# A fused attention and expert layer: state products in 32 by 32 pieces, scores a round earlier, half the keys turned outside TensorE, convolution taps shared by two engines

## The chip, the cores and the metric

The kernel runs on one core of a Trainium2 chip. The metric is the device time of one execution in microseconds (us); lower is better. The version before takes 1308.19 us, the median of three runs (1307.94 to 1309.42).

## The reference

The input is `x`, 8 sequences of 2048 tokens with 256 channels, in fp32. The output is `x` plus two branches that both read the normalised input.

```python
xn = layernorm(x)
# attention, 16 heads of 16, causal and linear (no softmax)
q, k, v = split(xn @ wqkv);  q, k = relu(q), relu(k)
kv  = cumsum(k[..., :, None] * v[..., None, :], axis=2)       # a 16x16 state per head
num = einsum('bhnd,bhnde->bhne', q, kv)
den = einsum('bhnd,bhnd->bhn', q, cumsum(k, axis=2)) + 1e-5
attn = (num / den) @ wo
# experts: top 2 of 8 by a sigmoid router; 4 are gated MLPs (256 -> 128 -> 256)
routed = sum_e cw[:, e] * ((silu(xn @ Wg[e]) * (xn @ Wu[e])) @ Wd[e])
routed += (cw[:, 4] + cw[:, 6]) * xn + cw[:, 7] * relu(xn)
shared = causal depthwise convolution of xn, 4 taps, + conv_b
out = x + attn + routed + shared
```

## The kernel before

**Tiling.** A sequence is cut into 4 batches of 512 tokens, a batch into 4 tiles of 128 tokens; there are 32 batches in all. The program is written out without loops on the chip: each engine has its own list of instructions in a fixed order, and semaphores tie the lists together. Nothing reorders the work but the order in which the code is written.

**One batch on TensorE.** `batch(s, j, left)` goes through these steps:

1. For each tile t: `gate_up(t)` (12 products of 512 columns) for expert t of all 512 tokens, then `numerators(t)`: a sum into the running state (`state_sum`, line 429), the masked scores times the values (line 466), another state sum, and the state times the query (line 482). After tile 0 the scores of the batch's tiles 2 and 3 are made (`scores(s, j, 0, 1)`, line 415).
2. `heads(s, j, 1)` makes values, keys and queries of the next batch, and turns its keys from channels by tokens into tokens by channels with eight 128 by 128 transposes (line 397) for the state sums. ScalarE copies them out to `ktok`.
3. For each tile, `output(t)`: the convolution turned back (line 488), attention times `wo`, hidden times `Wd`. Before tile 3 stand the scores of the next batch's tiles 0 and 1 (`scores(s, j, 1, 0)`) and its first state sum.

A weight or an input in fp32 is split in a high and a low part, so a matrix product is three passes (line 343). Products of attention (lines 415, 429, 466, 482) are plain fp32; the trace has each of these as two matmuls.

**PSUM.** Eight banks: four hold the scores (`SB[0..3]`, which also take the key and query projections and the transposes), three form a ring for everything in the tile loop, one holds the state. So scores can be written only when the masks of the scores before them are done.

**State times query.** Per 64 tokens the state is 256 channels by 16 for each head. VectorE's `blocks` (line 902) spreads it over a block-diagonal `state_bd` of 128 by 256, and TensorE multiplies it by `qT` in four products of 128 rows and 64 columns. `blocks` reads the state bank, so the next state sum waits for it (`s_bd`).

**Convolution.** From the fourth batch on, xn is turned in 32 by 32 blocks on VectorE (line 854) and the blocks are put in place by 32 small DMAs (SP, line 311), not by TensorE. The convolution starts with a ScalarE instruction pair (`first_tap`, line 654), and VectorE adds the other three taps with two multiply-adds each (line 916), after tiles 1, 2 and 3. TensorE needs the sum at `output(0)`.

**Engine queues.** ScalarE's list in a tile is `silu(t)`, `high_hid(t-1)`, `high_y(t)`. TensorE's `numerators(t)` waits for `silu(t)`, and `gate_up(t+1)` waits for VectorE's `hid` and `yT` of tile t. At the start of a batch TensorE's list also holds 38 waits on a semaphore that has long been set (`FILL`).

## Time and profile before

| | |
|---|---|
| median of 3 runs | 1308.19 us |
| the profiled execution, device time | 1308.92 us |
| its span (first to last instruction) | 1307.1 us |
| TensorE busy | 1287.2 us (98%) |
| VectorE busy | 1144.3 us (88%) |
| GpSimd busy | 830.8 us (64%) |
| ScalarE busy | 707.8 us (54%) |
| HBM traffic | 54 GB/s over the span |

The profiled execution is 1.8 us longer than its span and 0.7 us above the median. TensorE is written as PE (and PEld for its weight loads), VectorE as DVE, ScalarE as ACT, GpSimd as POOL and SyncE, which issues DMAs, as SP. In a timeline row the first number is the start, the second the length; rows of one kind are merged (x16 is sixteen instructions). A merged row's length reaches to the end of the last one, which is later than the start of the next row, since matmuls overlap; so steps are measured from start to start. "[0.54 <-X]" is idle time before a row and what ended it. A letter q behind an engine means its sequencer.

### The profile page before, as it was taken

What the parts mean: (1) busy time and instruction counts of PE and PEld (TensorE: products, weight loads), DVE (VectorE), ACT (ScalarE), POOL (GpSimd) and SP (SyncE); (2) the same over time, 40 slices, a digit from 0 to 9 for tenths busy, and PEclk for the clock granted to TensorE, in tenths of its full rate; (3) what the DMA queues carried; (4) which work ended last, traced back from release to release, by engine and by line L of the source; (5) the groups of instructions that cost most, each with busy time, mean ns of one, the idle gap of its engine ahead of it and who ended that gap; (6) DMA issues with size and microseconds to landing.
All of it is one profiled execution on the core that took longest, in us unless ns stands there. A gap on an engine that the chain in (4) does not pass through costs nothing.

```text
span 1307.1 us, 55818 instructions
## 1 busy us (share of the span) xinstructions
PE 1287.2 (98%) x24160; PEld 1116.5 (85%) x24160; DVE 1144.3 (88%) x2686; ACT 707.8 (54%) x1487; POOL 830.8 (64%) x673
## 2 busy tenths in 40 slices
PE   5999999999999999999999999999999999999998
PEld 4888888888888888888888888888888888888887
DVE  7988898888898888988888988889888889888885
ACT  5645655455654456554555544565545555445552
POOL 2676665765666756657656667566576566675554
PEclk9999999999999999999999999999999999999999
DMA  5012212222222222222222222221222222222211
GB/s 185 14 56 73 78 50 51 80 78 78 65 61 56 79 78 79 51 51 81 78 79 64 67 51 78 78 78 51 51 80 78 79 64 67 51 78 63 61 35 34
DMA packets 175860, 88.54 MB, mean 68 GB/s; under 512 B 135552, under 2 KB 171264, under 8 KB 171520
## 3 DMA queue, kind: packets, MB, share of 16 engines
q1 hardware_dynamic: 174912, 83.97, 22.6%
q8 instruction: 191, 3.13, 1.0%
q10 hardware_dynamic: 704, 1.01, 0.2%
q14 instruction: 53, 0.43, 0.1%
HBM read 53.18 MB, written 17.04 MB: 54 GB/s over the span
## 4 chain that ended last, share of the span: by engine, by line
PE 95%; DVE 3%; POOL 1%; issue 1%; ACT 0%; DMA 0%; DVEq 0%; POOLq 0%
PE ring L343 51%; PE scores L343 17%; PE ring L466 7%; PE ring L482 6%; PE scores L415 5%; PE state_sum L429 4%; PE ring L488 2%; PE scores L397 2%; DVE sm L895 1%; POOL xn L731 0%; DMA x_t<-in_L_attn_x_dram 0%; PE scores L352 0%; POOL rstd L722 0%; DVE stats L819 0%; POOL x_t L748 0%
## 5 line engine op out<-in xcount | busy, mean ns | idle before, releaser
L757 POOL TENSOR_TENSOR hid<-hid,cwb 128x512 f32<-128x512 f32 x128 | 166.4, 1300 | 181.8 <-DVE hid L924 181.0
L916 DVE SCALAR_TENSOR_TENSOR cT<-xT,conv_ws,cT 128x512 f32<-128x512 f32 x192 | 275.1, 1471 | 0.0
L745 POOL TENSOR_TENSOR x_t<-x_t,same 128x1024 f32<-128x1024 f32 x32 | 76.9, 2404 | 254.9 <-ACT same L618 254.9
L639 ACT ACTIVATE sg<-ring 128x512 f32<-128x512 f32 x128 | 76.6, 599 | 268.5 <-PE ring L343 268.5
L343 PE MATMUL ring<-xl,wgu_h 128*128 128x512 f32 x512 | 213.1, 416 | 0.0
L761 POOL TENSOR_TENSOR hl<-hid,hh 128x512 fp32r<-128x512 f32 x128 | 208.8, 1632 | 0.0
L343 PE MATMUL ring<-xh,wgu_l 128*128 128x512 f32 x512 | 201.0, 393 | 0.3 <-issue 0.3
L343 PE MATMUL ring<-xh,wgu_h 128*128 128x512 f32 x512 | 200.5, 392 | 0.0
L569 ACT ACTIVATE yh<-yT 128x256 fp32r<-128x256 f32 x128 | 53.5, 418 | 246.7 <-DVE yT L933 246.7
L902 DVE TENSOR_TENSOR state_bd<-state_sum,tables_s 128x256 f32<-128x256 f32 x248 | 104.0, 419 | 93.8 <-PE state_sum L429 90.6
L895 DVE TENSOR_TENSOR sm<-scores,causal_s 128x512 f32<-128x512 f32 x256 | 157.7, 675 | 6.0 <-PE scores L415 5.0
L343 PE MATMUL ring<-wd_l,hh 128*128 128x256 f32 x496 | 139.3, 281 | 0.0
L343 PE MATMUL ring<-wd_h,hh 128*128 128x256 f32 x496 | 139.1, 280 | 0.0
L343 PE MATMUL ring<-wd_h,hl 128*128 128x256 f32 x496 | 139.0, 280 | 0.0
L766 POOL TENSOR_TENSOR yl<-yT,yh 128x256 fp32r<-128x256 f32 x128 | 135.3, 1057 | 0.0
L466 PE MATMUL ring<-sm,vp 64*32 64x64 f32 x8192 | 122.2, 225 | 0.0
L343 PEld LDWEIGHTS ring<-xl,wgu_h 128*128 128x128 f32 x512 | 96.1, 188 | 26.1 <-issue 5.5
L343 PEld LDWEIGHTS ring<-xh,wgu_l 128*128 128x128 f32 x512 | 96.4, 188 | 23.1 <-issue 0.8
L343 PEld LDWEIGHTS ring<-xh,wgu_h 128*128 128x128 f32 x512 | 96.6, 189 | 16.6
L466 PEld LDWEIGHTS ring<-sm,vp 64*32 64x32 f32 x8192 | 101.6, 105 | 2.8 <-issue 2.8
L343 PE MATMUL scores<-xh,wqk_h 128*128 128x512 f32 x256 | 100.2, 392 | 0.0
L343 PE MATMUL scores<-xl,wqk_h 128*128 128x512 f32 x256 | 100.2, 391 | 0.0
(134 smaller groups left out, 3453.4 us busy)
## 6 DMA issues: line engine op xcount, KB each, us to landing
cwb<-cw_rows SPq DMA_DIRECT2D x32, 1024.0 KB, 4.6
x_t<-in_L_attn_x_dram SPq DMA_DIRECT2D x32, 512.0 KB, 4.2
out_dram<-x_t SPq DMA_DIRECT2D x31, 512.0 KB, 2.9
xT<-qks_tok SPq DMA_DIRECT2D x896, 16.0 KB, 1.8
cw_rows<-cwt SPq DMA_DIRECT2D x128, 2.0 KB, 1.4
sm<-in_L_attn_wqkv_dram ACTq DMA_DIRECT2D x2, 384.0 KB, 5.0
sm<-in_L_ffn_Wg_dram SPq DMA_DIRECT2D x2, 256.0 KB, 3.8
sm<-in_L_ffn_Wu_dram SPq DMA_DIRECT2D x2, 256.0 KB, 4.6
```

The source lines that it names most:

```text
L343: ins = mm(dst, lhs, rhs, start=first and n == 0, stop=final and n == len(passes) - 1, skip_group_check=not (first and final))
L415: ins = mm(SB[f][h * HALF:(h + 1) * HALF, at_:at_ + P], kT[rows, g, n0:n0 + HALF], qp[rows, g, :, n0:n0 + HALF], start=True, stop=True)
L466: mm(NB2[t % 2][h][BLK * m:BLK * m + BLK, gs], window, sm[toks, t // 2, t % 2, 2 * pair + par, :], start=par == 0 and g == 0, stop=False, ...
L482: ins = mm(NB2[t % 2][h][rows, g * HALF:(g + 1) * HALF], state_bd[:, n % 4, cols], qT[:, g, n0:n0 + HALF], start=False, stop=True, skip_gr ...
L639: act.activation(sg[:, :], GB[t % 2], ACT.Silu).then_inc(s_sg, 1)
L745: pool.tensor_tensor(xb, xb, same[:, :, :], ALU.add).then_inc(s_base1, 1)
L757: pool.tensor_tensor(hid[:, e, :], hid[:, e, :], cwb[:, e, :], ALU.mult).then_inc(s_hid, 1)
L761: pool.tensor_tensor(hl[:, e, :], hid[:, e, :], hh[:, e, :].bitcast(F32), ALU.subtract).then_inc(s_hl, 1)
L766: pool.tensor_tensor(yl[:, :, t * P:(t + 1) * P], yT[:, t % 2, :, :], yh[:, :, t * P:(t + 1) * P].bitcast(F32), ALU.subtract).then_inc(s_y ...
L895: dve.tensor_tensor(heads, SB[f][:, :].rearrange("p (t a n) -> p t a n", a=2, n=HALF), causal2_s[:, :].unsqueeze(1).unsqueeze(1).to_broadc ...
L902: dve.tensor_tensor(state_bd[:, n % 4, :].rearrange("p (g m n) -> p g m n", g=C, m=PPG), ST.unsqueeze(2).to_broadcast([P, C, PPG, BLK]), s ...
L916: ins = dve.scalar_tensor_tensor(out=cT[:, c, :], in0=xT[:, third(s, j, 0), c, LEAD - HALO + n:LEAD - HALO + n + BT], scalar=conv_ws[:, c, ...
```

## The change

1. **State times query.** `blocks` writes `state_ph`, 128 by 64: the state times a mask that separates the two heads of a pair. TensorE multiplies each 32 by 32 diagonal block on its own: 4 products per group of 128 channels and 64 tokens in place of 2. Each reads another 32 rows and writes another 32 partitions of one bank.
2. **Scores.** The scores of tiles 2 and 3 of a batch move from behind `numerators(0)` to behind the last `output(3)` of the batch before, and their masks on VectorE with them.
3. **Keys.** Of the eight key transposes, TensorE keeps the four of tiles 0 and 1. The other half is turned in 32 by 32 blocks by two VectorE instructions (`turn_keys`, into `hid[:, 2]`) and put in place by 16 small DMAs from SP. Three waits on `ktok_in` and `s_hl` guard this.
4. **Taps.** Where the next batch's xn goes by blocks, ScalarE multiplies (`tap_terms`, into the PSUM banks `SB[0:2]`) and VectorE only adds. The key projection, which uses these banks, now waits for `s_conv`.
5. **DMA issue.** Of the 32 DMAs that place xn, SP keeps 24; ScalarE issues 8, four behind each of two `tap_terms`.
6. The 38 waits (`FILL`) are removed.

```diff
-                            for w in range(2):
-                                rows = slice(w * HALF, (w + 1) * HALF)
-                                cols = slice(g * P + w * HALF, g * P + (w + 1) * HALF)
-                                ins = mm(NB2[t % 2][h][rows, g * HALF:(g + 1) * HALF], state_bd[:, n % 4, cols],
-                                         qT[:, g, n0:n0 + HALF], start=False, stop=True, skip_group_check=True)
+                            for m in range(PPG):
+                                rows = slice(BLK * m, BLK * m + BLK)
+                                ins = mm(NB2[t % 2][h][rows, g * HALF:(g + 1) * HALF], state_ph[rows, n % 4, g, :],
+                                         qT[rows, g, n0:n0 + HALF], start=False, stop=True, skip_group_check=True)
...
-                    for t in range(T):
+                    for t in range(T // 2 if k else T):
                         ins = nc.tensor.transpose(KTB[g][:, t * P:(t + 1) * P], kT[:, g, t * P:(t + 1) * P],
...
+                if k and by_blocks(s, j, k):
+                    pe.wait_ge(s_conv, at(s, j, HALO, HALO))
                 for g in range(C):
                     project(KB[g][:, :], D + g * P).then_inc(s_kp, 1)
...
+            def turn_keys(s, j, k):
+                for g in range(C):
+                    dve.wait_ge(s_kT, at(s, j, C, k * C + g + 1))
+                dve.wait_ge(s_hl, at(s, j, T, 3))
+                for t in range(2):
+                    ins = dve.transpose(kb[:, :, t, :, :].rearrange("p a g i -> p g a i"), ...
+                ins.then_inc(s_kturn, 1)
...
-                dve.tensor_tensor(state_bd[:, n % 4, :].rearrange("p (g m n) -> p g m n", g=C, m=PPG), ...
+                dve.tensor_tensor(state_ph[:, n % 4, :, :].rearrange("p g (a d) -> p g a d", a=2),
+                                  ST.rearrange("p g (a d) -> p g a d", a=2),
+                                  parity_s[:, :].unsqueeze(1).unsqueeze(3).to_broadcast([P, C, 2, HD]), ALU.mult
+                                  ).then_inc(s_bd, 1)
...
+                def tap_terms(n):
+                    if n == 1:
+                        act.wait_ge(s_sm, at(s, j, U * ROWS, U * ROWS))
+                    else:
+                        act.wait_ge(s_conv, at(s, j, HALO, n - 1))
+                    for c in range(C):
+                        first = LEAD - HALO + n
+                        ins = act.activation(TB[c][:, :], xT[:, third(s, j, 0), c, first:first + BT], ACT.Copy,
+                                             scale=conv_ws[:, c, n:n + 1])
+                    ins.then_inc(s_tapped, 1)
...
+                    for c in range(C):
+                        ins = dve.tensor_tensor(cT[:, c, :], TB[c][:, :], cT[:, c, :], ALU.add)
+                    ins.then_inc(s_conv, 1)
```

**The order on TensorE, from the last product of a batch to the second expert of the next.** `wd` rows end `output(3)`, `wgu` rows are `gate_up`, `scores` is line 415 (441 in the changed kernel). Before:

```order
L343 MATMUL ring<-wd_h,hl 128x256
L343 MATMUL ring<-xl,wgu_h 128x512 [waits tables_in,s_out]
...
L429 MATMUL state_sum<-vp,ktok 32x32 [waits s_bd]
L429 MATMUL state_sum<-vp,ktok 32x32 x7
L482 MATMUL ring<-qT,state_bd 64x64 [waits s_bd]
L482 MATMUL ring<-qT,state_bd 64x64 x3
L482 MATMUL ring<-qT,state_bd 64x64 [waits s_bd]
L482 MATMUL ring<-qT,state_bd 64x64 x3
L415 MATMUL scores<-qp,kT 64x128 [waits s_sm]
L415 MATMUL scores<-qp,kT 64x128 x31
L343 MATMUL ring<-xl,wgu_h 128x512 [waits s_gu]
```

In the changed kernel:

```order
L365 MATMUL ring<-wd_h,hl 128x256
L441 MATMUL scores<-qp,kT 64x128 [waits s_sm]
L441 MATMUL scores<-qp,kT 64x128 x31
L365 MATMUL ring<-xl,wgu_h 128x512 [waits s_out]
...
L458 MATMUL state_sum<-vp,ktok 32x32 [waits s_bd]
L458 MATMUL state_sum<-vp,ktok 32x32 x7
L510 MATMUL ring<-qT,state_ph 32x64 [waits s_bd]
L510 MATMUL ring<-qT,state_ph 32x64 x7
L510 MATMUL ring<-qT,state_ph 32x64 [waits s_bd]
L510 MATMUL ring<-qT,state_ph 32x64 x7
L365 MATMUL ring<-xl,wgu_h 128x512 [waits s_gu]
```

The 32 score products stand ahead of `gate_up(0)` instead of behind `numerators(0)`, and the group of 4 state products has become a group of 8.

**The order on VectorE, at the end of a batch and the start of the next.** `sm` rows are the masks of the scores, `x_t` rows add `output(t)`. Before:

```order
L976 TENSOR_TENSOR x_t<-ring,x_t 128x256 [waits s_op,s_base2]
L895 TENSOR_TENSOR sm<-scores,causal_s 128x4x128 [waits s_s]
L895 TENSOR_TENSOR sm<-scores,causal_s 128x4x128 x3
L902 TENSOR_TENSOR state_bd<-state_sum,tables_s 128x256 [waits s_st]
L976 TENSOR_TENSOR x_t<-ring,x_t 128x256 [waits s_op,s_base2]
L902 TENSOR_TENSOR state_bd<-state_sum,tables_s 128x256 [waits s_st]
```

In the changed kernel:

```order
L1060 TENSOR_TENSOR x_t<-ring,x_t 128x256 [waits s_op,s_base2]
L962 TENSOR_TENSOR sm<-scores,causal_s 128x4x128 [waits s_s]
L962 TENSOR_TENSOR sm<-scores,causal_s 128x4x128 x3
L969 TENSOR_TENSOR state_ph<-state_sum,tables_s 128x64 [waits s_st]
L1060 TENSOR_TENSOR x_t<-ring,x_t 128x256 [waits s_op,s_base2]
L962 TENSOR_TENSOR sm<-scores,causal_s 128x4x128 [waits s_s]
L962 TENSOR_TENSOR sm<-scores,causal_s 128x4x128 x3
L969 TENSOR_TENSOR state_ph<-state_sum,tables_s 128x64 [waits s_st]
```

A second set of masks now follows the last `x_t` of a batch, and the first set is what TensorE's moved scores wait for (`s_sm`).

**The order on ScalarE, in tiles 1 and 2 of a batch.** `sg` is `silu`, `hh` and `yh` are `high_hid` and `high_y`. Before:

```order
L639 ACTIVATE sg<-ring 128x512 [waits s_gu,s_gp]
L569 ACTIVATE hh<-hid 128x512 [waits s_hid]
L569 ACTIVATE yh<-yT 128x2x128 [waits s_y]
L639 ACTIVATE sg<-ring 128x512 [waits s_gu,s_gp]
L569 ACTIVATE hh<-hid 128x512 [waits s_hid]
```

In the changed kernel:

```order
L673 ACTIVATE sg<-ring 128x512 [waits s_gu,s_gp]
L592 ACTIVATE hh<-hid 128x512 [waits s_hid]
L701 ACTIVATE scores<-xT,conv_ws 128x512 [waits s_sm]
L701 ACTIVATE scores<-xT,conv_ws 128x512
L646 DMA xT<-qks_tok 32x4x32 [waits s_halo,s_turn]
L646 DMA xT<-qks_tok 32x4x32 x3
L592 ACTIVATE yh<-yT 128x2x128 [waits s_y]
L673 ACTIVATE sg<-ring 128x512 [waits s_gu,s_gp]
L592 ACTIVATE hh<-hid 128x512 [waits s_hid]
L701 ACTIVATE scores<-xT,conv_ws 128x512 [waits s_conv]
```

Two multiplications and four DMA issues stand between one `silu` and the next; here `scores` as an output is the bank in which the tap's product lies.

## Rows read from the trace of the kernel before

**Rows 1.** The page: busy time by engine, and the chain that ended last.

```profile
PE 1287.2 (98%) x24160; PEld 1116.5 (85%) x24160; DVE 1144.3 (88%) x2686; ACT 707.8 (54%) x1487; POOL 830.8 (64%) x673
PE 95%; DVE 3%; POOL 1%; issue 1%; ACT 0%; DMA 0%; DVEq 0%; POOLq 0%
```

**Rows 2.** One batch by windows: length, busy time of each engine, granted clock.

```profile
554.63:594.64 40.01, 40.01 (x763) 34.79 (x761) 36.00 (x86) 21.83 (x46) 26.06 (x22) 1.00 0.24 68
```

**Rows 3.** Timeline of TensorE, the key transposes and the first product behind them.

```profile
542.80 1.03 PE L397 MATMUL scores<-tables_s,kT 128*128 128x128 f32 x8
543.67 0.38 PE L488 MATMUL ring<-tables_s,cT 128*128 128x128 f32 x2
```

**Rows 4.** Timeline, the second state sum and VectorE's `blocks` ahead of it, tile 0.

```profile
557.52 0.24 PE L429 MATMUL state_sum<-vp,ktok 64*32 64x32 f32 x5
557.92 0.42 DVE L902 TENSOR_TENSOR state_bd<-state_sum,tables_s 128x256 f32<-128x256 f32 x1 [2.42 <-PE state_sum L429]
558.40 0.33 PE L429 MATMUL state_sum<-vp,ktok 64*32 64x32 f32 x16
558.65 0.69 PE L482 MATMUL ring<-qT,state_bd 128*64 128x64 f32 x16
559.27 1.21 PE L415 MATMUL scores<-qp,kT 32*64 32x128 f32 x64
```

**Rows 5.** Timeline of TensorE in tile 3, which has no second state sum.

```profile
572.78 0.24 PE L429 MATMUL state_sum<-vp,ktok 64*32 64x32 f32 x5
573.70 0.69 PE L482 MATMUL ring<-qT,state_bd 128*64 128x64 f32 x16
```

**Rows 6.** Groups of instructions by line and form: VectorE's and one of ScalarE's.

```profile
L916 DVE SCALAR_TENSOR_TENSOR cT<-xT,conv_ws,cT 128x512 f32<-128x512 f32 x192 | 275.1, 1471 | 0.0
L902 DVE TENSOR_TENSOR state_bd<-state_sum,tables_s 128x256 f32<-128x256 f32 x248 | 104.0, 419 | 93.8 <-PE state_sum L429 90.6
L924 DVE TENSOR_TENSOR hid<-ring,sg 128x512 f32<-128x512 f32 x128 | 87.0, 680 | 0.0
L654 ACT ACTIVATE cT<-xT,conv_bs,conv_ws 128x512 f32<-128x512 f32 x64 | 48.3, 804 | 0.0
```

**Rows 7.** Timeline of TensorE, from a batch's scores to the next batch.

```profile
550.82 1.21 PE L415 MATMUL scores<-qp,kT 32*64 32x128 f32 x64
554.63 0.42 PE L343 MATMUL ring<-xl,wgu_h 128*128 128x512 f32 x1
```

**Rows 8.** Timeline of VectorE and ScalarE, from the router to the masks, same batch.

```profile
538.70 0.23 ACT L601 ACTIVATE score<-ring 128x8 f32<-128x8 f32 x1
539.64 0.18 DVE L830 TENSOR_TENSOR scoreb<-score,bias_s 128x32 f32<-128x32 f32 x1
547.05 1.31 DVE L877 STREAM_TRANSPOSE qks_tok<-qks 128x512 f32<-128x512 f32 x2 [0.54 <-DMA xT<-qks_tok]
552.37 2.47 DVE L895 TENSOR_TENSOR sm<-scores,causal_s 128x512 f32<-128x512 f32 x4
```

**Rows 9.** Timeline: ScalarE's `silu` of tiles 0 to 2, one `yh`, SP's placing.

```profile
556.25 0.60 ACT L639 ACTIVATE sg<-ring 128x512 f32<-128x512 f32 x1 [4.98 <-PE ring L343]
561.17 24.11 SPq L311 DMA_DIRECT2D xT<-qks_tok  x32
562.10 0.60 ACT L639 ACTIVATE sg<-ring 128x512 f32<-128x512 f32 x1 [1.84 <-PE ring L343]
565.70 0.42 ACT L569 ACTIVATE yh<-yT 128x256 fp32r<-128x256 f32 x1 [2.48 <-DVE yT L933]
566.81 0.60 ACT L639 ACTIVATE sg<-ring 128x512 f32<-128x512 f32 x1 [0.70 <-PE ring L343]
```

**Rows 10.** A line's own answer: ScalarE's wait for `s_out` (its sequencer), one batch.

```profile
L652 ACTq EVENT_SEMAPHORE  x1: 17/17/17, 556.3 to 556.3; - x1
```

**Rows 11.** Timeline at the start of the program: first expert product, first masks.

```profile
29.16 0.79 PE L343 MATMUL ring<-xl,wgu_h 128*128 128x512 f32 x1
30.74 2.47 DVE L895 TENSOR_TENSOR sm<-scores,causal_s 128x512 f32<-128x512 f32 x4
```

89 lines of the change are left out of this document (67 added, 22 removed).

## The prediction

> **What bounds the kernel now.** I read the page first: TensorE is busy for 98% of the span, and 95% of the chain that ended last is its work [rows 1]. Then windows by batch: a middle batch takes 40.01 us, TensorE is busy for all of it at a granted clock of 1.00 (the 2.4 GHz level), while VectorE has 36.00, GpSimd 26.06 and ScalarE 21.83 us [rows 2]. So only three things count: what TensorE no longer executes, how long its small products take in their new shape, and whether somebody newly makes it wait. I then read its timeline from start to start, which shows waits that a busy share hides. VectorE's lighter load counts only where TensorE waits for it.
>
> **Keys (a saving).** Eight transposes take from 542.80 to 543.67, 0.87 us, or 0.109 each [rows 3]. Four go in each of the 31 batches that are prepared ahead: 31 x 4 x 0.109 = -13.5 us. Bounds: no more than this stretch would lose in proportion; down to -9 if a switch inside the stretch stays whole. The added work lies elsewhere: two VectorE block transposes of 256 elements, 0.35 us each by the 1.31 for two of 512 [rows 8], 0.7 us in all, and 16 DMAs. SP takes 24.11 us to issue 32 of the same small kind, 0.75 each [rows 9], so its list grows from 32 to 40 issues, 24 to 30 us, in a batch of 40. In time: placing starts 6.5 us into the batch (561.17 - 554.63) and now ends 18 us later, at 24.5; the routing weights are out at about 26 (the router's row is 24.9 into its batch, and it takes 3); their DMAs and 16 key DMAs take 15 more, to 41, which is 1 to 2 us into the next batch, some 5 before its placing begins. The keys are first read in that batch's tile 1. I cost this at nothing; beyond those 5 us each us of lateness is one of TensorE.
>
> **The state sums' hidden wait (a saving).** In tile 0 the first state sum starts at 557.52, `blocks` runs 557.92 to 558.34, the second state sum starts at 558.40 and the state products at 558.65: 1.13 us, of which the second sum is 0.25. The second sum starts 0.06 after `blocks` ends [rows 4]. Tile 3, without that second sum, needs 573.70 - 572.78 = 0.92 us [rows 5]. I take 0.1 to 0.13 of this for the switch to the next products' shape (an estimate: the scores too hold the next row back by more than their own pace), so TensorE could start the second sum after about 0.79, not 0.88. TensorE is thus waiting some 0.085 us for `blocks`, though its row shows no idle time. `blocks` shrinks from 256 to 64 elements: 419 ns at 256 and 680 at 512 [rows 6] give 1.02 ns an element, so about 0.22 us, 0.2 less. That is more than the 0.085, and the wait ends: 3 tiles x 32 batches x 0.085 = -8 us. Bounds 0 (the pace is set by something else) and -10.
>
> **State times query (same columns, twice the instructions).** The 16 matmuls take 558.65 to 559.27, 0.62 us [rows 4]: 8 steps of two side by side, 0.078 each with the ends. The new form has 32 matmuls of the same 64 columns, four side by side on four row and four column groups. If four run together, as the state sum's 16 do on four column groups (0.25 us [rows 4]), there are 8 steps again, and I add 0.013 for more starts (the scores' 64 in 1.21 us are 0.019 each at most): x 127 tiles = +1.7 us. Bounds: -0.05 per tile (smaller weight loads, -6 us) and, if the four follow one another, 4 x 0.62 = 2.48, +1.86 per tile, +236 us. I take the first, since the scores, also 32 rows high, need 1.21 us for 64 matmuls of 128 columns [rows 7], and so run several together. The scores' row groups each write a bank of their own, though; no row shows four row groups in one bank. The Trainium skill, "TensorEngine Tiling (Array Packing)", Gotcha 1, says that different row tiles cannot access the same PSUM bank simultaneously. By that rule the sum would be some 1530 us; it has a rival below.
>
> **Scores moved (nothing, and a new wait).** The 64 matmuls are the same. Their new place needs the masks of the scores before. In the frame of the scores' start S = 550.82, TensorE reaches the new place at 554.63 [rows 7], S + 3.8, or 3.9 with the change of shape. The masks take 2.47 [rows 8]. VectorE can start them at S + 1.25 at best, when the scores are out (their row's 1.21 and a semaphore), and they end at S + 3.72: no wait. But VectorE has to be free. In this batch it began at 552.37, S + 1.55 [rows 8]. Now: the taps' lighter work lets the router start when the score is out (538.93) instead of at 539.64, -0.7; the keys add 0.7; the 0.54 wait for the placing DMAs goes [rows 8]. The masks would start at 551.85. S itself comes 0.44 earlier by the transposes, at 550.38. So they start at S + 1.47, end at S + 3.94, and with 0.06 for the semaphore TensorE waits 0.12: x 31 = +3.7 us. Bounds 0 and +0.4 a batch (+12). Behind that wait stand `gate_up(0)` and all that follows, so nothing takes it up. The second masks then run beside `gate_up(0)` and are wanted in tile 2.
>
> At the start of the program the same move costs more. The first masks run 30.74 to 33.2, and `gate_up(0)` starts at 29.16 beside them [rows 11]. Now it stands behind the moved scores, which wait for these masks: 33.2 + 1.2 to 1.6 = 34.6, that is +5.5, of which 1.2 is given back after `numerators(0)` and about 1 in the wait for the masks there, which goes. +3 us, bounds +1 and +5.
>
> **Taps (off TensorE, one new wait).** VectorE's six multiply-adds (275.1/192 = 1.43 each, 8.6 us) become six adds with a PSUM operand (0.68, the form of line 924), 4.1 us [rows 6]. ScalarE gets six multiplications of at most 0.75 (48.3/64), 4.5 us. TensorE gains nothing. The key projection's new wait for the third tap: from `yT` of tile 3 the two adds need 1.3 us, and between them and the key projection TensorE has 24 value products of 264 columns, at 2.4 GHz at least 0.11 each, 2.6 us; covered by some 1 us.
>
> **DMAs on ScalarE (hidden, my main doubt).** Between `silu(1)` and `silu(2)` 4.71 us pass [rows 9]. ScalarE is idle for 2.48 and 0.70 of them, so it works for 1.53; the taps add 1.4 to 1.5: 3.0. Four DMA issues of 0.75 add 3.0. In one line this is 6.0 us, over the 4.71; with 0.6 per issue, 5.4. But ScalarE's sequencer went past its next wait at 556.3, while `silu` ran 556.25 to 556.85 [rows 9, 10]. It runs ahead, so the DMAs can be issued while the taps run, and be done before `yT` is there. I cost it at nothing. (The Trainium skill, "Advanced Engine Details and Errata", Engine Queue Depths, gives ScalarE a queue of 8. By this the two taps and `hh` fit, and the sum stays; the row shows a depth of one only.)
>
> The 38 removed waits: TensorE has no idle time at its batch's start, so they lay beside its queued work; -0.5 us, no more than -2.
>
> **Sum.** -13.5 - 8.0 + 1.7 + 3.7 + 3.0 - 0.5 = -13.6 us on the profiled execution's 1308.9 (span 1307.1 and 1.8 around it): 1295.3. The median is 0.7 lower: 1294.6.
>
> **Rivals.** A measurement of this kernel tells about 0.2% (2.6 us) from no change.
>
> 1. *ScalarE is the pacemaker of two tiles (slower).* For: 5.4 to 6.0 us in line against 4.71. `silu` ends at 556.85 and TensorE's state sum behind it starts at 557.52 [rows 4, 9], so 0.67 are in hand once. It decides as soon as the DMA issues start only after the taps have run. Price per batch: 2 x 0.7 - 0.67 = 0.7, up to 2 x 1.3 - 0.67 = 1.9; with 28 batches +20 to +53: 1315 to 1348, middle 1330; if the queue hides a part of it, from 1300 up. Against: the run ahead [rows 10]. Chance 0.15.
> 2. *Row groups queue at the bank (slower).* The four pieces of a step follow one another because they end in one bank; +236 us: about 1530. Against: each writes its own 32 partitions, and the state sum's four column groups share a bank at 0.25 us for 16 [rows 4]. Chance 0.04. (This is what the rule of Gotcha 1 of the Trainium skill's "TensorEngine Tiling (Array Packing)" would make of it.)
> 3. *The masks come late.* VectorE's chain loses another 0.3 us a batch, by slower strided transposes or by waits for keys: +9, and 1304. For: VectorE ends nearest to the bound of all. Against: it loses about 5 us of work a batch. Chance 0.13.
> 4. *More is gained.* State products with small weight loads and no wait at the masks: -6 and -4, and 1285. Chance 0.08.
>
> The forecast has 0.60: 1294.5, with a range of its own of 1288 to 1301. The range for 8 in 10 takes in most of rivals 3 and 4 and the lower part of rival 1: 1284 to 1314. Faster by over 0.2%: the forecast, rival 4 and nearly all of rival 3, 0.79. Within 0.2%: the rest of rival 3 and the least of rival 1, 0.04. Slower: 0.17.
>
> **What would show it.** After: four key transposes in about 0.43 us; the first state sum to the state products at about 1.05, not 1.13; state products still 0.62 to 0.65 from start to start; TensorE idle by 0.1 at the moved scores, put down to VectorE's mask; a batch near 39.4 us. If instead `silu(2)` and `silu(3)` start later behind ScalarE's DMAs and TensorE's first state sums of tiles 2 and 3 wait for `sg`, rival 1 holds. If state products take 2 us, rival 2.

## Result: slower, and what the profile after shows

The changed kernel takes **1331.99 us** (median of 4 runs, 1329.99 to 1332.55) against 1308.49 on the same chip: a ratio of **1.0176, 95% interval 1.0158 to 1.0194**. The prediction said 1294.5, with a range of 1284 to 1314. It was wrong by 37.5 us and in its sign.

The page of the profile after: busy times, then three of its DMA queues (packets, MB, share), then the chain that ended last.

```profile
PE 1295.3 (97%) x26020; PEld 1113.7 (84%) x26020; DVE 1006.2 (76%) x2748; ACT 796.6 (60%) x1655; POOL 754.6 (57%) x673
q1 hardware_dynamic: 214080, 88.44, 25.2%
q10 hardware_dynamic: 32960, 4.69, 2.0%
q8 instruction: 204, 3.34, 1.1%
PE 91%; DVE 5%; issue 2%; POOL 1%; ACT 1%; DMA 0%; ACTq 0%; DVEq 0%; POOLq 0%
```

VectorE has become lighter, as planned. GpSimd has too (830.8 us before), which nothing in the plan meant: it executes the same 673 instructions, but the mean one of its `hl` products takes 1337 ns and took 1632. TensorE's share of the chain has fallen from 95% [rows 1], and "issue", time in which an engine waits for nothing that the profile shows, has gone from 1% to 2%.

What I had predicted of tile 0 and of the key transposes came true. Timeline of a tile 0 and of the key transposes (start, us, engine, line, count):

```profile
494.25 0.25 PE L458 MATMUL state_sum<-vp,ktok 64*32 64x32 f32 x5
494.65 0.23 DVE L969 TENSOR_TENSOR state_ph<-state_sum,tables_s 128x64 f32<-128x64 f32 x1 [0.79 <-PE state_sum L458]
495.28 0.65 PE L510 MATMUL ring<-qT,state_ph 32*32 32x64 f32 x32
...
559.12 0.60 PE L423 MATMUL scores<-tables_s,kT 128*128 128x128 f32 x4
559.55 0.38 PE L516 MATMUL ring<-tables_s,cT 128*128 128x128 f32 x2
```

First state sum to state products: 1.03 us (1.13 in [rows 4]; 1.05 predicted). `blocks` takes 0.23. The 32 state products are as long as the 16 before. Rival 2 is out. (The Trainium skill, "TensorEngine Tiling (Array Packing)", Gotcha 1, says that different row tiles cannot access the same PSUM bank simultaneously; these 0.65 us show no cost of such a rule for pieces that write different partitions.) Four transposes take 0.43 instead of eight in 0.87 [rows 3].

But the same stretch in tiles 1 and 2 looks different. Timeline of tile 1 in a later batch, TensorE with ScalarE's DMA issues:

```profile
537.57 0.60 ACT L673 ACTIVATE sg<-ring 128x512 f32<-128x512 f32 x1 [0.68 <-PE ring L365]
537.80 0.60 ACTq L646 DMA_DIRECT2D xT<-qks_tok  x1
...
538.82 0.24 PE L458 MATMUL state_sum<-vp,ktok 64*32 64x32 f32 x5
539.34 1.39 ACTq L646 DMA_DIRECT2D xT<-qks_tok  x2
539.88 0.50 PE L458 MATMUL state_sum<-vp,ktok 64*32 64x32 f32 x16
540.31 0.84 PE L510 MATMUL ring<-qT,state_ph 32*32 32x64 f32 x32
```

1.49 us instead of 1.03, and the products 0.84 instead of 0.65, without a wait on any row. `silu` was not late: ScalarE's sequencer issued the first DMA while `silu` ran, as I had assumed. That is the first finding. The second: there are single long pauses. TensorE at the end of a tile 0:

```profile
575.82 0.65 PE L510 MATMUL ring<-qT,state_ph 32*32 32x64 f32 x32
577.81 0.50 PE L365 MATMUL ring<-xl,wgu_h 128*128 128x512 f32 x1 [1.34 <-issue]
```

The table takes TensorE's starts of the 24 batches from the sixth on (mean us of each stage, to the start of the next):

| | before | after |
|---|---|---|
| first `gate_up(0)` / sixth batch begins | 29.16 / 235.02 | 36.18 / 245.39 |
| batch | 39.95 | 40.54 |
| small stage of tile 0, 1, 2, 3 | 1.69, 1.75, 1.75, 1.53 | 1.69, 2.17, 2.05, 1.53 |
| the four gate stages | 11.75 | 11.96 |
| key transposes | 0.87 | 0.43 |
| second scores (in tile 0 / at the end) | 1.14 | 1.14 |

(Small stage: from the first state sum to the next gate product.) So 10.4 of the 23.5 us are lost by the sixth batch and 14.0 in the next 24; 0.9 come back in the last two and at the end.

**The clock.** The prediction took TensorE's clock as 1.00 throughout. Inside the span it was granted at 0.50 (1.2 GHz) for 3.4 us before and for 13.7 us after: 27.7 to 37.9, and again 252.9 to 256.3, 1.3 us after a pause of 1.65 us had ended. Three stretches of TensorE by windows (length, busy time, granted clock, DMA), the first from the kernel before, the others from the changed one (the moved scores, and the first gate products behind them):

```profile
29.16:31.30 2.14, 2.14 (x12) 0.50 0.91 368
34.23:36.18 1.95, 1.95 (x65) 0.50 0.00 0
36.18:37.90 1.72, 1.72 (x12) 0.50 0.00 0
```

From start to start a gate product takes 0.24 us ahead of 252.9 and 0.43 behind it. So each us at this level costs a busy TensorE about half a us (an estimate from these rows): 1.7 us for the later stretch.

**A count that the profile does not print.** In the program each TensorE matmul is two instructions (load, multiply). With the waits the program of before has 49,088 and the changed one 52,307. Queue 8 on the page carried 191 and 204 packets of 16,384 bytes: one per 256 instructions (191.8 and 204.3). So these packets are TensorE's own instructions, fetched while it runs; one takes 0.9 to 1.8 us. I matched each matmul of a trace with its place in the program. In the changed kernel (after the first 60 us) 10 gaps of over 0.44 us stand ahead of instruction 197 or 198 of a block of 256; all other gaps stand ahead of an instruction that waits for another engine. At each of the 10 the newest fetch landed between 1.0 us before and 0.3 us after the gap's start (575.19 to 576.40 for the one above). They sum to 9.3 us. Before there is one, 0.5 us. (The place depends on where one starts to count: from the kernel's own first instruction it is 193 or 194.)

The end of a pause tells more than its start. Over all twenty traces there are 172 pauses ahead of an instruction that has no wait of its own. Each ends 1.10 to 1.65 us after the landing of its block's fetch (the k-th fetch for the k-th block; mean 1.40, standard deviation 0.10), while its start lies anywhere from 1.5 us before the landing to 1.5 us behind it. And at none of some 3,800 block ends does the instruction at this place start sooner than 1.09 us after the landing. So a pause lasts until its fetch has landed and 1.4 us more have passed, and a block end without a pause is one whose fetch had landed early enough.

### The profile page after: what moved, and what is told of

It is laid out like the page before. It is cut to its first block, busy times and chain, and to the rows that moved or that the text cites. A ratio compares the mean times of both kernels' runs of the same rounds, so it can differ in the third digit from the quotient of the medians.

```text
span 1330.8 us, 59962 instructions
## 1 busy us (share of the span) xinstructions
PE 1295.3 (97%) x26020; PEld 1113.7 (84%) x26020; DVE 1006.2 (76%) x2748; ACT 796.6 (60%) x1655; POOL 754.6 (57%) x673
## 4 chain that ended last, share of the span: by engine, by line
PE 91%; DVE 5%; issue 2%; POOL 1%; ACT 1%; DMA 0%; ACTq 0%; DVEq 0%; POOLq 0%
PE ring L365 49%; PE scores L365 16%; PE ring L495 7%; PE ring L510 6%; PE scores L441 5%; PE state_sum L458 4%; PE ring L516 2%; PE scores L423 1%; DVE cT L997 1%; DVE ksum L929 1%; DVE sm L962 1%; DVE stats L876 0%; DMA x_t<-in_L_attn_x_dram 0%; POOL xn L788 0%; DVE qks_tok L944 0%
## 5 line engine op out<-in xcount | busy, mean ns | idle before, releaser
L969 DVE TENSOR_TENSOR state_ph<-state_sum,tables_s 128x64 f32<-128x64 f32 x248 | 55.1, 222 | 185.6 <-PE state_sum L458 185.0
L818 POOL TENSOR_TENSOR hl<-hid,hh 128x512 fp32r<-128x512 f32 x128 | 171.2, 1337 | 0.0
L495 PE MATMUL ring<-sm,vp 64*32 64x64 f32 x8192 | 128.0, 225 | 0.0
L495 PEld LDWEIGHTS ring<-sm,vp 64*32 64x32 f32 x8192 | 106.3, 105 | 4.1 <-issue 3.0
L701 ACT ACTIVATE scores<-xT,conv_ws 128x512 f32<-128x512 f32 x168 | 108.7, 683 | 0.0
L458 PEld LDWEIGHTS state_sum<-vp,ktok 64*32 64x32 f32 x3968 | 65.3, 106 | 50.7 <-issue 47.9
L985 DVE TENSOR_TENSOR cT<-scores,cT 128x512 f32<-128x512 f32 x168 | 107.4, 680 | 0.0
L823 POOL TENSOR_TENSOR yl<-yT,yh 128x256 fp32r<-128x256 f32 x128 | 98.8, 772 | 3.0 <-ACT yh L592 2.1
```

The costliest lines, as they stand in the source:

```text
L458: ins = mm(ST[rows, g, :], ktok[toks, t, g, rows], vp[toks, t, g * PPG + m, 0:3:2, :], start=first and g == 0, stop=True, skip_group_check ...
L495: mm(NB2[t % 2][h][BLK * m:BLK * m + BLK, gs], window, sm[toks, t // 2, t % 2, 2 * pair + par, :], start=par == 0 and g == 0, stop=False, ...
L701: ins = act.activation(TB[c][:, :], xT[:, third(s, j, 0), c, first:first + BT], ACT.Copy, scale=conv_ws[:, c, n:n + 1])
L818: pool.tensor_tensor(hl[:, e, :], hid[:, e, :], hh[:, e, :].bitcast(F32), ALU.subtract).then_inc(s_hl, 1)
L823: pool.tensor_tensor(yl[:, :, t * P:(t + 1) * P], yT[:, t % 2, :, :], yh[:, :, t * P:(t + 1) * P].bitcast(F32), ALU.subtract).then_inc(s_y ...
L985: ins = dve.tensor_tensor(cT[:, c, :], TB[c][:, :], cT[:, c, :], ALU.add)
```

## The experiments

Theories: **A**, DMA issues on ScalarE slow TensorE's small products. **P** (first called B), the ends of 256-instruction blocks matter by where they fall. **C**, the start pays for the moved scores. In all tables "batch" is the mean of the same 24 batches in us, "pauses" are gaps over 0.44 us at places 197 and 198, number and sum in the profiled run, and "small 1, 2" the small stages of tiles 1 and 2, median us.

### First: one part undone or done alone

`u1_all_sp`: `place_turned(s, j, 2, 1, range(QUADS))` on SyncE, both calls on ScalarE removed.

> The changed kernel with one part undone: all 32 DMAs of a batch that place the turned query are issued by SyncE again, none by ScalarE. Theory A (ScalarE issuing DMAs is what stretches TensorE's small products in tiles 1 and 2, 28 batches by 0.8 us): about 1308 us, and from the state sum to the state products 1.03 us in tiles 1 and 2 as in tile 0. Theory B (TensorE runs short of instructions because there are now more of them in its densest stretch and the row of 38 waits is gone; who issues DMAs does not matter): 1330 us, tiles 1 and 2 as slow as in the changed kernel.

`b1_act_dmas`: in the kernel before, SyncE's loop is cut and ScalarE gets the changed kernel's calls:

```diff
-                    for a in range(QUADS):
+                    for a in range(QUADS if c == 0 else QUADS // 2):
...
+                if left > 1 and by_blocks(s, j, 2):
+                    place_turned(s, j, 2)
                 high_y(1)
```

> The kernel before with one part of the change alone: 8 of the 32 placing DMAs (the last two quarters of the second half) issued by ScalarE, four in tile 1 and four in tile 2. Theory A: 28 batches by 0.8 us more, 1308 + 22 = 1330 us, or a little less where the wait for the diagonal blocks (0.1 us a tile) takes part of it up. Theory B: 1308 us within 0.3%.

`u2_wide_state`: `state_bd` and the 128x64 products back in the changed kernel.

> The changed kernel with the first part undone: the state times the query as 128x64 products on a state written out in diagonal blocks again, everything else as changed. Theory A: 8 us lost on the wait for the blocks (0.1 us a tile in tiles 0 to 2) unless the slow tiles hide it, so 1332 to 1340 us. Theory B (more small products are what starves TensorE): faster than 1332, about 1315 us, with tiles 1 and 2 at 1.13 us from the state sum to the state products, as before.

`u3_fill38`: the changed kernel with

```diff
+                if not last and by_blocks(s, j, 1):
+                    for _ in range(38):
+                        pe.wait_ge(tables_in, 16)
                 for t in range(T):
                     gate_up(t)
```

> The changed kernel with the 38 satisfied waits ahead of tile 0 put back on TensorE's queue. Theory A: 1332 us within 0.3% (they cost at most 2 us and gain nothing). Theory B (the place of small products in the instruction stream decides which stretch is late): 1310 to 1322 us, the single pauses of 0.9 to 1.9 us gone.

| | us | ratio to before, 95% | batch | small 1, 2 | pauses |
|---|---|---|---|---|---|
| u1_all_sp | 1382.95 | 1.0526 to 1.0574 | 42.43 | 1.68, 1.68 | 12, 11.0 |
| b1_act_dmas | 1318.70 | 1.0059 to 1.0093 | 40.28 | 1.95, 1.98 | 1, 0.2 |
| u2_wide_state | 1324.86 | 1.0103 to 1.0137 | 40.27 | 2.02, 2.00 | 0 |
| u3_fill38 | 1388.79 | 1.0585 to 1.0628 | 42.62 | 2.21, 2.07 | 10, 13.6 |

A holds in the stage it names: off ScalarE, the small stages fall to 1.68; put there in the kernel before, they rise by 0.2 each, with nothing else changed, for 9.5 us. I had given b1 22 us: a stage with wide products suffers less (0.2 a tile) than one with 32x32 products (0.4 to 0.5). The wide products themselves keep their 0.62 us in b1 and u2; the delay stands ahead of them. The 32x32 ones stretch too, from 0.58 to about 0.76 (medians from start to start). With all 48 DMAs on SyncE the total gets worse by something else. Its chain, and TensorE's first waits:

```profile
SPq 61%; PE 17%; DMA 7%; DVE 7%; issue 6%; POOL 1%; ACT 0%; DVEq 0%; POOLq 0%
...
PE scores L441 <- DVE sm L958: 52.9, 29, 4.1
```

SyncE's list is then longer than a batch, VectorE waits for the placing (3.76 us in one batch) and the moved scores for the masks. u2 fits neither theory as I had put them (1332 to 1340, or 1315): the pauses are gone and tiles 1 and 2 are still slow (2.02 and 2.00). The 38 waits in u3 fell through both: instead of 1332 or 1310 to 1322 it became 1389, with 1.9 us from the last score to the first gate product in the 28 batches that have them (0.2 without). Behind the moved scores, which are short products, TensorE's sequencer has little lead, and the waits cost nearly their full time.

### Second: which part brings the pauses

`b2_small_state`: the kernel before with `state_ph` and the 32x32 products. `u4_scores_old`: in the changed kernel `scores(s, j, 0, 1)` and its `mask` back in tile 0. `u6_nokeys_sp`: eight transposes again, no key DMAs, all placing on SyncE.

> The kernel before with the first part of the change alone: the state times the query as 32x32 products, all DMAs on SyncE, scores and the 38 waits in their old place. My prediction's terms for this part: 8 us less (the 0.1 us wait for the blocks in tiles 0 to 2) and 1.7 more for the products, 1302 us. Theory B (the doubled number of instructions in the small stage meets the instruction fetch at times): the small stage of tiles 1 and 2 shorter by 0.07 us, but pauses of 0.5 to 3 us at single fetches as in the changed kernel, 10 us in sum, 1308 to 1315 us.

> The changed kernel with the second part undone: the last two tiles' scores and their masks back in tile 0 of their own batch, the rest as changed. Theory C (the move costs the program's start and the first batches, 10 us by the fifth batch, and nothing in a steady batch): 1322 us, first gate product near 29 us. Rival (the move costs in the steady batch too, through the wider alignment of the instruction stream): below 1318 or above 1327 us.

> The changed kernel with two parts undone: all eight key transposes on TensorE, no key DMAs, and all 32 placing DMAs on SyncE. (With the placing on SyncE and the 16 key DMAs there too, 1383 us, SyncE's queue was 61% of the chain: this leaves it as long as before.) Theory A: small stages of tiles 1 and 2 at 1.68 us with no DMAs on ScalarE; 1332 - 28 x 0.95 + 31 x 0.44 = 1319 us; nothing of VectorE's 3.8 us wait for the placing. Rival (the slow small stages come from the taps that ScalarE and VectorE share through PSUM): tiles 1 and 2 at 2.1 us or more, 1340 us or more.

`u7_timed`: ScalarE's DMAs each behind a wait for the state products of a tile:

```diff
+                act.wait_ge(s_num, at(s, j, T, t))
...
+                place_turned(s, j, 2, range(2))
                 high_y(1)
...
+                place_turned(s, j, 4, range(4, 8))
                 high_y(3)
```

> The changed kernel with ScalarE's 8 DMAs at another time: each group waits for the end of the state products of tile 1 (two), 2 (two) and 3 (four), so that they are issued beside the gate and head products instead of beside the small ones. Theory A, in the form that only the small products suffer: tiles 1 and 2 back at 1.68 us in their small stage, 0.95 x 28 us less, 1307 us, or some 3 us more where the heads' copies on ScalarE come late behind four DMAs. Rival (any DMA on ScalarE's queue costs TensorE 0.12 us, whenever it is issued): 1330 us, with the gate stages of tiles 2 and 3 and the head stage longer instead.

| | us | ratio, 95% | batch | small 1, 2 | pauses |
|---|---|---|---|---|---|
| b2_small_state | 1332.64 | 1.0160 to 1.0203 | 40.90 | 1.69, 1.69 | 25, 29.5 |
| u4_scores_old | 1349.09 | 1.0269 to 1.0315 | 41.62 | 2.11, 2.10 | 28, 39.1 |
| u6_nokeys_sp | 1334.54 | 1.0186 to 1.0225 | 40.71 | 1.67, 1.69 | 12, 9.5 |
| u7_timed | 1474.88 | 1.1242 to 1.1279 | 45.93 | 1.69, 1.67 | 15, 15.5 |

b2 is the sharpest: **one part of the change, without any DMA moved, loses 23.4 us, as much as the whole**, though its tiles 1 and 2 are faster than before by 0.07 each. I had expected some 10 us of pauses; there are 29.5. TensorE within a row of scores:

```profile
565.03 0.92 PE L415 MATMUL scores<-qp,kT 32*64 32x128 f32 x41
567.56 0.66 PE L415 MATMUL scores<-qp,kT 32*64 32x128 f32 x23 [1.61 <-issue]
568.15 0.50 PE L343 MATMUL ring<-xl,wgu_h 128*128 128x512 f32 x1
```

Half way through 64 equal products, with all operands there, TensorE stops for 1.6 us. u4 shows what moving the scores is worth beside 32x32 products. With the scores in tile 0 the dense stretch is longer, and 15 of its 28 pauses stand in the scores, where the changed kernel has none. Although the start is won back (29.8 us to the first gate product, sixth batch at 237.9), it loses 17 us. Five stretches at the lower clock (17.1 us after the first 60 us of the run, where the changed kernel has 3.4) are part of that. My theory C alone (1322) missed it. u6 again has fast tiles without ScalarE's DMAs, but waits 0.5 us more at the moved scores, and came out 15 us above my estimate. u7 was meant to give 1307 and is the slowest of all. Behind explicit waits ScalarE has no run ahead and holds up VectorE; TensorE then waits for VectorE's masks and hardly for `silu`. Some of its waits (us in total, times, longest):

```profile
ACT yh L592 <- issue: 182.8, 59, 5.1
DVE scoreb L890 <- ACT score L624: 90.4, 29, 6.0
PE scores L441 <- DVE sm L965: 50.1, 31, 3.9
PE state_sum L458 <- ACT sg L677: 1.6, 6, 0.6
```

So this is a late ScalarE as in rival 1 of the prediction, but along another path. And the clock was at its lower level for 133 us of this run against 13.7 in the changed kernel, which explains about 60 of the 143 us between the two (an estimate at half a us for each): u7 therefore does not tell what the timing of the DMAs alone is worth.

### Third: the waits as the only variable

`b3_nofill` removes the 38 waits from the kernel before. `b4_bad_fill` only changes their number:

```diff
-    FILL = 38
+    FILL = (48, 20, 38, 80)
-                    for _ in range(FILL):
+                    for _ in range(FILL[j]):
```

> The kernel before without its 38 satisfied waits ahead of tile 0, nothing else. In the traces so far every single pause of TensorE above 0.5 us that waits for nothing (11 in the changed kernel, 27 with 32x32 products alone) stands at the 197th or 198th instruction of a block of 256 of TensorE's program, with a 16,384-byte fetch of instructions (256 of 64 bytes) just landed. Theory P (place in the stream): the 38 waits, 19 instructions a batch, hold four batches at 6135 instructions, near 24 x 256, so that block ends drift slowly and stay clear of the scores and the end of tile 0's small stage; without them block ends sweep over those, 15 times in the program, at 0.5 to 1.4 us each: 1309 + 7 to 21, so 1323 us. My prediction's own term: the waits cost up to 2 us, so 1307 to 1309 us.

> The kernel before with its 38 waits a batch replaced by 48, 20, 38 and 80 in the four batches of a sequence (46 on average), chosen so that a block end (every 256th instruction, at 198) falls into tile 0's scores or the last 16 small products before them in 32 places instead of 2. No instruction that computes anything changes. Theory P: 30 more pauses of 0.5 to 1.4 us, 1325 to 1350 us, middle 1340. Rival (the waits act by their number only, or not at all): 1309 us within 0.3%.

`p1_after_pads`: such waits (76, 40, 66, 72) in the changed kernel ahead of `output(1)`. `m3_keys_act_late`: a version made from the findings, whose parts are listed in what was expected; 8 key DMAs go behind `denominators(s, j, 1)` on ScalarE.

> The changed kernel with satisfied waits (76, 40, 66 and 72 in the four batches of a sequence) put between the first and second output product, where TensorE's products are long, chosen so that no block end falls near the end of a small stage, the scores or the gate product behind them. Theory P: the single pauses are gone (10 us in sum) and the slow small stages of tiles 1 and 2 stay, 1322 us; the waits cost nothing there, or up to 0.1 us an instruction as they did in front of tile 0 (32 of them a batch: 3 us a batch, 1410 us). Rival (pauses come at random with the fetch's own duration): 1332 us or more, as many pauses as before.

> A version made from the findings: key halves turned in blocks and the taps split as in the changed kernel, the state times the query as 128x64 products again, scores and masks in the old place, all 32 placing DMAs on SyncE, and 8 of the 16 key DMAs on ScalarE's queue, behind its last head work, beside the output products; 64, 54, 32 and 66 waits ahead of tile 0, which keep block ends away from tile 0's scores. Theory: as before minus the keys (0.44 us a batch), 1309 - 13 = 1296 us, as long as SyncE's placing (32 DMAs) lands before VectorE needs the place; rival: VectorE waits for the placing and masks come late as with everything on SyncE, 1300 to 1320 us.

| | us | ratio, 95% | batch | small 1, 2 | pauses |
|---|---|---|---|---|---|
| b3_nofill | 1318.22 | 1.0059 to 1.0093 | 40.36 | 1.75, 1.75 | 10, 8.7 |
| b4_bad_fill | 1365.44 | 1.0411 to 1.0451 | 41.89 | 1.75, 1.75 | 25, 28.3 |
| p1_after_pads | 1368.08 | 1.0439 to 1.0481 | 41.69 | 2.19, 2.05 | 12, 7.5 |
| m3_keys_act_late | 1324.02 | 1.0100 to 1.0134 | 40.48 | 1.75, 1.75 | 0 |

Fewer waits are slower (by 9.3 us) and more waits are slower (by 56.6): not their number but where they put the block ends. b3 came out 5 us under my estimate and b4 25 over it, since b4 has two more effects beside its 28.3 us of pauses: 14 gaps in front of `gate_up(0)`, 19.7 us in sum, and three stretches at the lower clock (10.2 us, so about 5.1 lost), each beginning between 0.2 us before and 1.2 us after the end of one of these gaps. Together 53.1 of the 56.6 us. One row of each kind. A pause in the scores, and a gap in front of the first gate product:

```profile
495.29 0.97 PE L415 MATMUL scores<-qp,kT 32*64 32x128 f32 x47
497.62 0.48 PE L415 MATMUL scores<-qp,kT 32*64 32x128 f32 x17 [1.36 <-issue]
...
490.61 0.47 PE L343 MATMUL ring<-xl,wgu_h 128*128 128x512 f32 x1 [2.10 <-issue]
```

The gap grows with the waits in one place (two waits make one instruction): from start to start nothing to see at 19, then 0.60 us at 24, 0.92 at 27, 1.47 at 32, 1.60 at 33, 2.42 at 40, in b4 and m3 together. That is 0.114 us an instruction beyond some 20, behind long output products; TensorE's lead there is about 20 x 0.114 = 2.3 us (an estimate from this slope). (The Trainium skill, "Advanced Engine Details and Errata", Engine Queue Depths, gives TensorE a queue of 64. By this an estimate of the lead, for 64 instructions or 32 output products at 0.12, would be 3.8 us; the runs show less.) This took p1's gain and m3's: p1 had up to 38 instructions in one place (2.1 us from start to start there), m3 up to 33. I had named that risk for p1 and not for m3.

### Fourth: the same, with the waits covered

`p2_after_split` has p1's waits in two places, ahead of `output(1)` and `output(2)`. `u8_late_keys` adds m3's DMA arrangement to it. `m4_split` is m3 with at most 17 instructions in a place, `m2_keys_act_late` is m3 without waits.

> The changed kernel with the same number of satisfied waits as in the first padded version (38, 20, 33 and 36 instructions in the four batches of a sequence), half ahead of the second output product and half ahead of the third, so that no place has more than 19. In the first padded version 33 to 38 instructions at one place cost 1.6 to 2.1 us and 20 cost nothing. Theory P: no pauses at the 198th instruction of a block of more than 1 us, waits covered, 1332 - 10 = 1322 us, tiles 1 and 2 still at 2.2 and 2.05 us. Rival (any wait costs 0.1 us): 1332 - 10 + 90 = 1410 us.

> The same kernel (changed, waits split), and in it all 32 placing DMAs on SyncE and 8 of the 16 key DMAs on ScalarE behind its last head work, beside the output products: SyncE issues as many as in the changed kernel, ScalarE too, but none in tiles 1 and 2. Theory A: small stages of tiles 1 and 2 at 1.68 us, 28 x 0.9 = 25 us less than with the waits alone, 1297 us, plus 0.3 to 0.6 us a batch (8 to 17 us) where the masks of the first two tiles now come late for the moved scores, as they did with the placing on SyncE: 1305 to 1314 us. Rival (ScalarE's DMAs cost TensorE wherever they are issued): 1322 us or more, output stage longer by 0.9 us.

> The version with the key halves, 128x64 state products, scores and masks in the old place, placing on SyncE and late key DMAs on ScalarE (1324 us with 16 to 33 wait instructions in one place, of which the trace showed 0.9 to 1.6 us a batch uncovered and no pauses at block ends), with its waits split into two places of at most 17. Theory: 1324 - 28 x 0.95 = 1297 us, 1% faster than before, the batch 39.5 us. Rival (the waits were not what lengthened the gate of tile 0 and the gap ahead of it): 1324 us.

> The same version with no waits at all. Theory P: block ends fall into tile 0's scores or the gate behind them in 15 places, as in the kernel before without its waits (there 9 us by 14.7 such places): 1297 + 9 = 1306 us. Rival (the pauses need something that this version lacks): 1297 us.

| | us | ratio, 95% | batch | small 1, 2 | pauses |
|---|---|---|---|---|---|
| p2_after_split | 1324.15 | 1.0098 to 1.0129 | 40.27 | 2.22, 2.08 | 5, 3.4 |
| u8_late_keys | 1330.59 | 1.0137 to 1.0197 | 40.41 | 1.67, 1.64 | 10, 8.3 |
| **m4_split** | **1301.58** | **0.9927 to 0.9954** | 39.54 | 1.75, 1.75 | 0 |
| m2_keys_act_late | 1317.48 | 1.0047 to 1.0077 | 40.31 | 1.75, 1.75 | 11, 14.4 |

p2 against the changed kernel: 7.8 us less time, 5.9 us less in pauses, and 1.7 for the later stretch at the lower clock, which p2 does not have. m4 against m2: 15.9 us less, 14.4 less in pauses, and again 1.7 for one such stretch (each pause of m2 is longer than in b3, so it came out 11 us over my estimate; m4 itself 5). u8: tiles 1 and 2 in the same kernel fall by 0.55 and 0.44 once ScalarE issues nothing there. Timeline of its tile 2:

```profile
541.37 0.24 PE L458 MATMUL state_sum<-vp,ktok 64*32 64x32 f32 x5
542.40 0.65 PE L510 MATMUL ring<-qT,state_ph 32*32 32x64 f32 x32
```

1.03 us again. What this won went into a wait (us in total, times, longest):

```profile
PE scores L441 <- DVE sm L970: 25.1, 21, 3.9
```

With the placing on SyncE, VectorE's masks are late for the moved scores; and u8 has five pauses more than p2, with TensorE's program the same. By the landings above, pauses come and go with how early each fetch lands before its block end is reached; what sets that was not tested. It ended 17 us above the upper end that I gave; the mechanism held and the total did not.

m4 beats the kernel before by 7.3 us. Its page and one of its batches by windows (length, busy times of TensorE, its loads, VectorE, ScalarE, GpSimd, clock):

```profile
PE 1272.5 (98%) x24036; PEld 1102.3 (85%) x24036; DVE 1048.0 (81%) x2748; ACT 797.4 (61%) x1655; POOL 756.5 (58%) x673
PE 95%; DVE 3%; issue 1%; POOL 1%; ACT 0%; DMA 0%; DVEq 0%; POOLq 0%
...
434.81:474.44 39.63, 39.63 (x759) 34.39 (x758) 32.35 (x87) 25.22 (x52) 23.35 (x22) 1.00 0.32 78
```

39.54 us a batch is 0.41 less than before: the key transposes' 0.44. Not all of it reaches the total: by the sixth batch m4 is 1.2 us behind (236.26 against 235.02).

### Last: the taps

`m6_taps_dve` gives m4's three taps back to VectorE whole; `m7_taps_dve_nowait` also makes TensorE's `pe.wait_ge(s_conv, ...)` ahead of the key projection a satisfied one.

> The version of 1301.6 us with the three taps computed whole on VectorE again (one part undone, TensorE's instructions the same to the last). My prediction's term (the split moves nothing on the path): 1301 us within 0.3%, small stages of tiles 1 and 2 at 1.75 us either way. Rival (VectorE's longer taps delay the router, the placing's successor and the masks of the first two tiles, so that the state sum of the next tile 0 or the scores wait): 1303 to 1310 us, with a wait for VectorE in front of tile 0's small stage in most batches instead of 4.

> The version with the taps whole on VectorE, and the wait for them ahead of the key projection replaced by a satisfied wait (they are still waited for ahead of the first output product). My prediction's term (the split moves nothing on the path): 1301 us within 0.3%, the 0.67 us gap ahead of the key projection gone. Rival (VectorE's longer stretch of taps comes out again further on, at the masks or the placing): the gap moves and 1305 us or more stay.

m6: 1315.11 us (1.0036 to 1.0069), with steps of 0.67 us at the key projection, where TensorE still waits for the taps, a wait that only the split needs. m7: 1308.77 us (0.9993 to 1.0013), batch 39.86, so the split is worth 7.2 us in m4. The reason is not the taps' own place. ScalarE and then TensorE in m7, at the start of a batch:

```profile
509.66 0.26 ACT L679 ACTIVATE dene<-den 128x64 f32<-128x64 f32 x1 [0.54 <-DVE den L953]
509.67 6.37 ACTq L661 DMA_DIRECT2D ktok<-hid  x8
516.07 1.28 ACT L688 ACT_TABLE_LOAD   x1 [6.15 <-issue]
517.36 0.60 ACT L688 ACTIVATE sg<-ring 128x512 f32<-128x512 f32 x1
...
516.96 0.39 PE L365 MATMUL ring<-xh,wgu_l 128*128 128x512 f32 x1
518.06 0.25 PE L458 MATMUL state_sum<-vp,ktok 64*32 64x32 f32 x7 [0.71 <-issue]
```

VectorE with full taps hands over `den` later: ScalarE's `dene` starts 5.05 us ahead of the first gate product in m4 and 4.43 in m7, the issue of its last key DMA ends 0.4 us after that product's start in m4 and 1.18 in m7 (means of 25 batches). ScalarE's eight key DMAs and a table load then push `silu(0)` behind the gate products, and TensorE waits: 17 such gaps of 12.3 us in sum ahead of state sums in m7, 7 of 5.9 us in m4. The lighter VectorE is the cover of m4's late DMAs.

## Why the prediction was wrong, by its steps

Two steps failed in kind. "DMAs on ScalarE", which I cost at nothing, is some 25 us by the lengths of the stages. And I priced only the time of instructions, never their number: with "-0.5" for the 38 waits and "+1.7" for twice the state products, the block ends were left out, which are 9.3 us of pauses in the changed kernel and 23.4 us in b2. A third step, the start of the program at "+3", was too small: +10.4 by the sixth batch. The parts:

- **Keys, -13.5 us**: right in size on TensorE (0.44 x 31), and shown by m4's batch; of this m4's total shows 7.3.
- **The hidden wait, -8, and state products, +1.7**: right where nothing disturbs them, rather better: medians of the four small stages in u8 are 1.61, 1.67, 1.64 and 1.50 against 1.75, 1.75, 1.75 and 1.53 before, 0.36 a batch or 11 us. Unseen was what 32 matmuls in place of 16 do to the *instruction stream*. "Same columns, twice the instructions" counted the array's time alone; b2 puts the part at +23.4 us instead of -6.3.
- **The 38 removed waits, -0.5**: this step failed in sign and kind. I priced what they cost and did not ask what they were for. They held four batches at 6135 instructions, 9 short of 24 x 256, and so kept block ends away from the scores; without them the kernel before loses 9.3 us (b3). I never counted instructions, though the page's 191 instruction packets were there to be read.
- **Scores moved, +3.7 in steady batches**: too much; there the wait is absent (the moved scores take 1.14 us as in their old place), and what is left is 0.08 a batch in the last `output(3)`, 2.50 against 2.42. At the start, "+3, bounds +1 and +5", it was +7.0 to the first gate product and 10.4 by the sixth batch. Timeline:

```profile
29.62 0.44 PE L458 MATMUL state_sum<-vp,ktok 64*32 64x32 f32 x16
34.23 2.02 PE L441 MATMUL scores<-qp,kT 32*64 32x128 f32 x64 [4.18 <-DVE sm L962]
36.18 0.80 PE L365 MATMUL ring<-xl,wgu_h 128*128 128x512 f32 x1
```

  The masks end at 34.2, not at 33.2 as in [rows 11], and the scores behind that idle time take 1.95 us, where I had allowed 1.2 to 1.6: TensorE's clock is at 0.50 until 37.9, while in the kernel before it is back at 1.00 from 31.3. In the first three batches, where VectorE still has more to do, the moved scores waited 1.2 us and more each time (first at 77.0). u4, with the scores back, has its sixth batch at 237.9 instead of 245.4. Yet the move also shortens the dense stretch of tile 0, and is worth 17 us net with 32x32 products (u4 against the changed kernel, the clock included).
- **DMAs on ScalarE, nothing**: my main doubt, with the wrong mechanism. The run ahead is real and `silu` is on time; but TensorE's small products stretch while ScalarE issues. Medians of 2.22 and 2.09 against u8's 1.67 and 1.64 are 1.0 a batch, 28 us in the 28 batches that have them; by the means, 2.17 and 2.05, it is 25. No run shows this in its total: b1 lost 9.5 us with wide products, and u8 gave the time back elsewhere. Rival 1 named the right place and, by chance, the right total (middle 1330); its sign, `silu` late, did not appear, so I do not count it as having happened.
- **Taps, nothing**: the wait ahead of the key projection is covered, as said; the lighter VectorE is worth something only where a late ScalarE needs it.

The sum from the table of stages, which counts nothing twice: 10.4 us by the sixth batch; in the 24 batches behind it 24 x (0.42 + 0.30) = 17.3 in tiles 1 and 2 (DMAs, and the pauses that fall there), 24 x 0.21 = 5.0 in the gate stages, 24 x 0.08 = 1.9 in the last output and 24 x -0.44 = -10.6 for the keys, together 13.6 of the 14.0; then -0.9. What each part does alone does not add up to this: b2 alone loses 23.4 us and b1 9.5, since where pauses fall depends on the whole program.

**Open.** Why issuing on ScalarE slows TensorE's small products was not shown: only that it does, by tile, in both directions, and that SyncE's issues do not. That the pauses depend on the place in the block of 256 is shown by b3, b4, m2 and m4, and that each ends with the landing of a fetch by the 172 pauses; what fills the 1.4 us between landing and next instruction, and what decides when a fetch starts, is open. No run changed the clock alone, so what it costs is an estimate.

## What to carry to other kernels

Where an engine runs at 98% with stretches of very short instructions, count its instructions as well as its time: find the fetches on the page, see in which stretch each block of 256 ends, and treat odd padding (satisfied waits) as a part of the schedule. Here padding cost nothing only where the engine had a lead, behind long instructions. And before moving small DMAs to a compute engine's queue, look at what TensorE does while they are issued, not only at that engine's own list.

## What the hardware did that I had not expected

- TensorE stopped for up to 2.3 us (up to 2.8 in u3) between two equal products, at place 197 or 198 of a 256-instruction block. In before, after, b3, m2 and m4 no gap of over 0.44 us within a row of equal products stands anywhere else.
- Block ends inside 128x64 state products never paused it (some 9 of them in u2 and 15 in b4); in the scores behind them they did (b3, m2: 0.6 to 1.8 us from start to start), and more with 32x32 products.
- TensorE's clock fell to 0.50 in the middle of a run 58 times in these traces, and each time next to the end of an idle gap of TensorE (1.56 to 2.79 us long; its end lay between 1.7 us before the fall and 0.3 us after it). The reverse does not hold: 81 gaps of over 1.5 us, some of 2.27 in u1, brought no fall.
- A satisfied pair of waits on TensorE takes 0.114 us once its lead is used up, as much as an output product of 256 columns (0.12).
- A DMA issue took about as long on ScalarE (0.59 to 2.05 us, median 0.67, mean 0.76) as on SyncE (0.59 to 2.04, median 0.60, mean 0.71; the 0.75 of [rows 9] is a pace of this kind). What differed was what it did to TensorE.
